# Single attention on one Trainium2 core: the input's statistics one batch further ahead, and its norm moved in front of the residual updates on VectorE

## The reference, cut to what matters

```python
def _layernorm(x, axis=-1, eps=1e-05):
    m = jnp.mean(x, axis=axis, keepdims=True)
    v = jnp.var(x, axis=axis, keepdims=True)
    return (x - m) / jnp.sqrt(v + eps)
...
    q = jnp.einsum('bld,de->ble', query, Wq) + bq
    k = jnp.einsum('bld,de->ble', key, Wk) + bk
    v = jnp.einsum('bld,de->ble', value, Wv) + bv
    scores = jnp.einsum('bqe,bke->bqk', q, k)
    attn = jax.nn.softmax(scores, axis=-1)
    out = jnp.einsum('bqk,bke->bqe', attn, v)
...
    x = _layernorm(x + _L1_attn_ref(x, ...), axis=-1)
    x = _layernorm(x + _L1_xattn_ref(x, ctx_512, ctx_512, ...), axis=-1)
    x = _layernorm(x + _L1_ffn_ref(x, ...), axis=-1)
```

## Time and profile before

| | us |
|---|---|
| median of 3 runs | 2440.24 (2439.1 to 2442.52) |
| the profiled execution, its own time | 2441.61 |
| its span, first to last instruction | 2439.6 |
| PE busy in the span | 2228.2 (91%) |
| VectorE busy | 1570.2 (64%) |
| ScalarE busy | 1121.4 (46%) |
| GpSimd busy | 886.8 (36%) |
| start of the stage's first norm (`E_xn`) and of its last offsets (`E_minus`) | 1935.80 and 2129.07 |
| first instruction of VectorE in the next stage (route) | 2132.88 |

### The profile page before, as it was taken

One profiled execution on the slowest core, in us unless ns is written; L12 is line 12 of the kernel. 1 busy time (PEld: TensorE's weight loads), 2 busy tenths in 40 slices (PEclk: granted clock), 3 DMA queues, 4 the chain that ended last, 5 costly groups with the idle time before them and its releaser, 6 DMA issues. The chain is left out here.

```text
span 2439.6 us, 54300 instructions
## 1 busy us (share of the span) xinstructions
PE 2228.2 (91%) x20297; PEld 1517.8 (62%) x20392; DVE 1570.2 (64%) x3365; ACT 1121.4 (46%) x2397; POOL 886.8 (36%) x1263
## 2 busy tenths in 40 slices
PE   8989999999999997989999999999999699759996
PEld 6656666666666664556666666566666577636664
DVE  2368888788878884746667666666766477652222
ACT  3333333333333331156666666666666277712221
POOL 2111111111111100036666666665665367632442
PEclk9999999999999998989999999999999699959998
DMA  4200000000000001300000000000000022232330
GB/s 147 72 2 2 0 0 0 0 0 0 0 0 0 0 1 50 97 14 0 0 0 0 0 0 0 0 0 0 0 0 1 1 69 89 96 106 91 104 107 24
DMA packets 53289, 65.35 MB, mean 27 GB/s; under 512 B 6257, under 2 KB 46150, under 8 KB 53240
## 3 DMA queue, kind: packets, MB, share of 16 engines
q1 hardware_dynamic: 50168, 56.60, 7.3%
q0 software_dynamic: 3072, 8.07, 1.0%
HBM read 44.01 MB, written 20.97 MB: 27 GB/s over the span
## 5 line engine op out<-in xcount | busy, mean ns | idle before, releaser
L392 PE MATMUL B_ps_s<-B_xk,B_xT 128*32 128x308 f32 x4096 | 278.1, 423 | 9.1 <-DVE B_xk L658 9.1
L1556 DVE TENSOR_TENSOR D_att<-D_ps_s,D_dexp 128x1024 f32<-128x1024 f32 x128 | 154.6, 1208 | 131.2 <-PE D_ps_s L1225 73.3
L413 PE MATMUL B_ps_m<-B_wo,B_oT 128*128 128x256 f32 x1024 | 235.3, 386 | 2.1 <-ACT B_oT L551 2.1
L1126 POOL TENSOR_SCALAR_AFFINE_SELECT D_att<-D_att 128x1024 f32<-128x1024 f32 x128 | 139.9, 1093 | 250.3 <-DVE D_att L1556 250.3
L392 PEld LDWEIGHTS B_ps_s<-B_xk,B_xT 128*32 128x32 f32 x4096 | 129.7, 109 | 142.1 <-issue 13.1
L413 PEld LDWEIGHTS B_ps_m<-B_wo,B_oT 128*128 128x128 f32 x1024 | 192.2, 191 | 39.6 <-issue 12.8
L519 ACT ACTIVATE B_prob<-B_prob 128x616 f32<-128x616 f32 x128 | 92.9, 726 | 241.9 <-DVE B_prob L630 241.9
L308 POOL TENSOR_TENSOR B_veps<-B_mv,eps 128x2 f32<-128x2 f32 x32 | 6.2, 195 | 508.7 <-DVE B_mv L612 508.7
L1134 POOL TENSOR_TENSOR D_orms<-D_oms,D_half 128x32 f32<-128x32 f32 x32 | 174.0, 5436 | 2.7
L1225 PE MATMUL D_ps_s<-D_q2T,D_kT 32*128 32x256 f32 x1024 | 147.7, 404 | 3.7 <-DVE D_att L1556 3.7
L628 DVE TENSOR_REDUCE B_mx<-B_ps_s 128x8 f32<-128x616 f32 x128 | 100.1, 782 | 64.0 <-PE B_ps_s L392 64.0
(11 more groups left out here) (317 smaller groups left out, 4942.8 us busy)
## 6 DMA issues: line engine op xcount, KB each, us to landing
res<-in_x SPq DMA_DIRECT2D x16, 512.0 KB, 3.5
x_d<-res SPq DMA_DIRECT2D x8, 1024.0 KB, 4.5
wi<-in_L_ffn_wi SPq DMA_DIRECT2D x8, 1024.0 KB, 5.0
wo<-in_L_ffn_wo SPq DMA_DIRECT2D x8, 1024.0 KB, 7.5
out<-E_fin SPq DMA_DIRECT2D x7, 1024.0 KB, 7.1
C_wgu<-in_L_ffn_gate_up SPq DMA_DIRECT2D x8, 512.0 KB, 3.6
C_wdn<-in_L_ffn_down_proj SPq DMA_DIRECT2D x8, 256.0 KB, 2.8
B_wqT<-in_L_xattn_WqT SPq DMA_DIRECT2D x1, 1024.0 KB, 11.0
```

The source lines that it names most:

```text
L392: last = nc.tensor.matmul(ps_s[u % 2][q * G:(q + 1) * G, g, 0:HQ * S], xT[:, par, k, (2 * u + g) * G:(2 * u + g + 1) * G], xk[:, par, k].r ...
L413: last = nc.tensor.matmul(ps_m[:, bank, 0:D], oT[:, m, t * P:(t + 1) * P], wo[:, m], start=m == 0, stop=m == MT - 1)
L1126: nc.gpsimd.affine_select(out=att[:, n % 2], in_=att[:, n % 2], compare_op=ALU.is_ge, fill=0.0, base=0, pattern=[[0, HT], [1, P]], channel ...
L1556: nc.vector.tensor_tensor(att[:, n % 2].rearrange("p h i -> p (h i)"), ps_s[:].rearrange("p a n -> p (a n)"), dexp[:, n % 2], ALU.mult).th ...
```

## The change

The statistics of the input are taken at batch b+4, and aggregated and scaled at b+3, where both were at b+2. Input and output statistics get a semaphore each (`stats`, `stats_out`). The first halves of `st` and `mv` are rewritten behind explicit waits: the statistics wait for the last aggregation (`aggr`), the aggregation waits for the norm that still reads `mv` (`xn_ready`). The norm of b+2 moves from the end of VectorE's step to a place in front of the aggregation, ahead of `invert_sums` and `add_out`. GpSimd's order is the same with `norm_scale` numbered one further. Batch 2 gets its aggregation and scales, and batch 3 its statistics, in the prologue. The loop covers steps 3 to 27, and two more steps are written out.

```diff
--- before.py
+++ after.py
@@ -1724,8 +1724,8 @@
         s_out = ps_s[:, 0:NT * (S + E)].rearrange("p (t s) -> p t s", t=NT)
         g_sum, g_v, g_bias, g_bv = (ps_o[:, 1, 64 * n:64 * n + E] for n in range(4))
 
-        set_ready, bias_ready, stats, seen, aggr, var_eps, rstd_ready, xn_ready, resid_ready, ctx_ready = map(
-            sem, "set_ready bias_ready stats seen aggr var_eps rstd_ready xn_ready resid_ready ctx_ready".split())
+        set_ready, bias_ready, stats, stats_out, seen, aggr, var_eps, rstd_ready, xn_ready, resid_ready, ctx_ready = map(
+            sem, "set_ready bias_ready stats stats_out seen aggr var_eps rstd_ready xn_ready resid_ready ctx_ready".split())
         xT_done, k_done, kq_done, v_done, s_done, pT_done, o_done = map(
             sem, "xT_done k_done kq_done v_done s_done pT_done o_done".split())
         gated_ready, g_sum_done, gate_ready, g_v_done, g_v_ready = map(
@@ -1739,12 +1739,12 @@
 
         def steps(engine, body):
             def parts(b):
-                return dict(att=b < B, nxt=b + 1 < B, nxt2=b + 2 < B, sums=1 <= b <= B, x5=2 <= b <= B + 1)
+                return dict(att=b < B, nxt=b + 1 < B, nxt2=b + 2 < B, nxt3=b + 3 < B, nxt4=b + 4 < B, sums=1 <= b <= B, x5=2 <= b <= B + 1)
             for b in range(3):
                 body(b, **parts(b))
-            with engine.Fori(3, B - 2) as b:
-                body(b, att=True, nxt=True, nxt2=True, sums=True, x5=True)
-            for b in range(B - 2, B + 2):
+            with engine.Fori(3, B - 4) as b:
+                body(b, att=True, nxt=True, nxt2=True, nxt3=True, nxt4=True, sums=True, x5=True)
+            for b in range(B - 4, B + 2):
                 body(b, **parts(b))
 
         @block.sync
@@ -1794,13 +1794,13 @@
                 pool.wait_ge(xn_ready, b + 1)
                 nc.gpsimd.tensor_copy(res[:, b], xn[:]).then_inc(resid_ready, 1)
 
-            def body(b, att, nxt, nxt2, sums, x5):
+            def body(b, att, nxt, nxt2, nxt3, nxt4, sums, x5):
                 if nxt2:
                     stage_context(b + 2)
-                if nxt2 or sums:
-                    norm_scale(b + 2, 0 if nxt2 else 1, 2 if sums else 1)
+                if nxt3 or sums:
+                    norm_scale(b + 3, 0 if nxt3 else 1, 2 if sums else 1)
                 if sums:
-                    x5_scales(b - 1, b + 2, first=not x5)
+                    x5_scales(b - 1, b + 3, first=not x5)
                 if nxt2:
                     keep_residual(b + 2)
 
@@ -1814,6 +1814,7 @@
                 norm_scale(b, 0, 1)
                 keep_residual(b)
             stage_context(1)
+            norm_scale(2, 0, 1)
             steps(pool, body)
 
         @block.tensor
...
@@ -1962,16 +1963,23 @@
 
         @block.vector
         def _(dve):
-            def norm_stats(first, last_of):
-                for i, b in enumerate((first, last_of)):
-                    if b is not None:
-                        for t in range(NT):
-                            last = nc.vector.bn_stats(st[:, i, t], res[:, b, t])
-                last.then_inc(stats, 1)
-
-            def norm_aggregate(n, first, last_of):
-                dve.wait_ge(stats, n + 1)
-                dve.sem_inc(seen)
+            def norm_stats(i, b, done):
+                if i == 0 and not (isinstance(b, int) and b == 0):
+                    dve.wait_ge(aggr, b)
+                for t in range(NT):
+                    last = nc.vector.bn_stats(st[:, i, t], res[:, b, t])
+                last.then_inc(done, 1)
+
+            def norm_aggregate(first, last_of):
+                if first is not None:
+                    dve.wait_ge(stats, first + 1)
+                    dve.sem_inc(seen)
+                    if not (isinstance(first, int) and first == 0):
+                        dve.wait_ge(xn_ready, first)
+                        dve.sem_inc(seen)
+                if last_of is not None:
+                    dve.wait_ge(stats_out, last_of + 1)
+                    dve.sem_inc(seen)
                 for i, b in enumerate((first, last_of)):
                     if b is not None:
                         for t in range(NT):
@@ -2018,27 +2026,27 @@
                 nc.vector.scalar_tensor_tensor(minus[:], mv[:, 1, :, 0].unsqueeze(1).to_broadcast([P, 3, NT]), -1.0, scale_n[:],
                                                ALU.mult, ALU.mult).then_inc(minus_ready, 1)
 
-            def body(b, att, nxt, nxt2, sums, x5):
+            def body(b, att, nxt, nxt2, nxt3, nxt4, sums, x5):
                 if att:
                     maxima(b)
-                batches = (b + 2 if nxt2 else None, b - 1 if sums else None)
                 if sums:
                     dve.wait_ge(res_ready, b * NT)
-                if nxt2 or sums:
-                    norm_stats(*batches)
+                    norm_stats(1, b - 1, stats_out)
                 if x5:
                     x5_offsets(b - 2, first=att and b == 2 if isinstance(b, int) else False)
                     dve.wait_ge(minus_ready, b - 1)
-                if nxt2 or sums:
-                    norm_aggregate(b + 2, *batches)
+                if nxt2:
+                    norm_apply(b + 2)
+                if nxt3 or sums:
+                    norm_aggregate(b + 3 if nxt3 else None, b - 1 if sums else None)
                 if att:
                     invert_sums(b)
+                if nxt4:
+                    norm_stats(0, b + 4, stats)
                 if att:
                     add_out(b)
                 if nxt:
                     copy_v(b + 1)
-                if nxt2:
-                    norm_apply(b + 2)
 
             dve.wait_ge(w_loaded, LOADED)
             nc.vector.tensor_tensor(gated[:], gateT[:], gammaT[:].unsqueeze(2).to_broadcast([P, KD, E]), ALU.mult).then_inc(gated_ready, 1)
@@ -2051,9 +2059,12 @@
             dve.wait_ge(gate_ready, 1)
             nc.vector.tensor_copy(kq[:, :, S:S + E], gate[:]).then_inc(bias_ready, 1)
             for b in range(2):
-                norm_stats(b, None)
-                norm_aggregate(b, b, None)
+                norm_stats(0, b, stats)
+                norm_aggregate(b, None)
                 norm_apply(b)
+            norm_stats(0, 2, stats)
+            norm_aggregate(2, None)
+            norm_stats(0, 3, stats)
             dve.wait_ge(g_v_done, 1)
             nc.vector.tensor_copy(wv[:, D:D + E], g_v)
             nc.vector.tensor_copy(bv[:, D:D + E], g_bv[0:S])
```

## The result

The changed kernel takes 2456.34 us (median of 4 runs, 2455.97 to 2457.68), the kernel before 2440.72 us in the same session (4 runs, 2439.1 to 2442.52): a ratio of 1.0064, 95% interval 1.0051 to 1.0077. It is slower, as predicted, but by 15.6 us where 6.8 were forecast, and 2456.3 lies above the range of 2442.0 to 2451.5. The profiled execution took 2457.68 us, span 2455.9 us (before 2439.6).

A forecast was written before the change was run, and what follows sets the result against it. The order of hand-overs, not one engine's work, bounded the 5.61 us step. A new ring of 4.75 + 0.24 + 0.72 + 0.24 = 5.95 us, run 28 times, gave +6.8 us on 2440.24: 2447.0 us, range 2442 to 2451.5.

The forecast's parts named there:

- The bubble: PE's wait of 0.49 us a step for VectorE's normed input, before the input transposes; moving the norm would close it.
- The chain that is left: PE's chain from scores to next scores, 5.42 us a step; if nothing else held, each step would gain 0.19 us.
- a ring through GpSimd: Norm, aggregation, GpSimd's whole step, next norm, in the attention loop: 5.95 us a step, above PE's chain of 5.42.
- the signs named beforehand: Scores every 5.9 us, PE's norm wait gone, its exponential wait larger, GpSimd's aggregation wait 1.3 to 1.5, VectorE newly waiting on GpSimd.
- The tail behind the norm of step 29: After the last ring: norm and hand-over, four chains of aggregation to scales, three hand-overs back; 17.4 us.
- L(1): Start of the norm of step 1, moved from 1951.37 to 1952.33 behind the maxima and two statistics.
- that copy's end to the norm's start: Ring term from the end of GpSimd's residual copy to VectorE's norm: 0.24 us taken, bounds 0.04 and 0.24.
- The second way round: Ring through GpSimd's scales and VectorE's offsets to the norm, 6.09 us or more; rival at +10 to +14 us, 10%.
- Written-out steps: Three ring steps outside the loop, both hand-overs short: 5.75 us each, 17.25 us in the sum.
- The first steps: Attention steps up to about the third would be shorter than 5.6 us.
- The rule on semaphores: If semaphores cost nothing, the non-binding ring would be the forecast; the sum instead followed the trace's 0.15 and 0.24 us gaps.
- The rival on the other side: Hand-overs cost nothing, ring 5.40 us under PE's 5.42, bubble gone: 5.3 us faster, 2435 us; chance 4%.

The follow-up runs named there:

- the kernel with both moves: Changed kernel with GpSimd's residual copy moved in front of the reciprocal root and the norm moved in front of the offsets on VectorE; 2437.88 us, ratio 0.9985.
- the kernel with the copy first: Changed kernel with only GpSimd's residual copy moved from the end of its step to in front of the reciprocal root; 2452.41 us, ratio 1.0051.
- the last kernel: Changed kernel, residual copy first but waiting until the offsets are written, norm ahead of the offsets; 2433.23 us with the loop, 2431.26 us with it written out.
- the kernel with both moves and the copy kept away: Changed kernel, norm ahead of the offsets, residual copy at the head of GpSimd's step but waiting until the offsets are written; 2433.23 us, ratio 0.997.

## Why the prediction was right in direction and wrong in size

**What bounded the kernel before: right.** TensorE's chain, with VectorE's norm in it, set the step there. Writing its loop out gained nothing, and one more power on GpSimd cost 0.11 us a step.

**The bubble: right.** PE's wait for the normed input is gone. The chain that is left was put at 5.42 us; where nothing else binds it is 5.29 us. The term that was off is the copy of K: I took its whole 0.54 us, but its two instructions overlap what follows. In the kernel with both moves the scores start at 1966.06, the copy at 1968.08, the exponential at 1968.51, the transposes of the probabilities at 1969.29 and the next scores at 1971.36: 2.02 + 0.43 + 0.78 + 2.07 = 5.30.

**That a ring through GpSimd binds: right, shown by the runs.** One more power on GpSimd costs 0.53 us a step after the change, 0.11 before it. Its first term, aggregation to the end of the residual copy, was 4.75 us, as predicted. Of the signs named beforehand, VectorE's wait for PE is gone, the new wait stands in front of the offsets, and PE's wait for the exponentials, in no row before, is 8.9 us, as ScalarE's wait for the maxima grew from 5.3 to 20.2 us. The scores come every 6.34 us, not every 5.9; GpSimd's wait for the aggregation, put at 1.3 to 1.5 us a step, is 1.87. The tail behind the norm of step 29 was put at 17.4 us and measured 17.38 (2128.68 to 2146.06); the start, L(1), at 1952.33 and measured 1952.44. All the error lies between: 176.24 us for the 28 rings where the sum has 166.00.

**The step that failed** is "that copy's end to the norm's start ... so I take 0.24". The norm is not the next thing behind the copy. It is the token copy and the offsets, which no semaphore ties to the residual copy, but which end with it. From the copy's end to the norm it is therefore 0.01 + 0.07 + 0.51 = 0.59 us in the loop, 0.35 more than the sum has. With 0.02 on the norm (0.74 for 0.72) and 0.03 on the last hand-over (0.27 for 0.24) that is, but for rounding, the 0.39 us between 6.34 and 5.95. The prediction calls this a ring "with nothing in parallel to it"; scales and offsets lie in parallel to the residual copy, and they bind.

**The second way round** (6.09 us), which I had as the upper bound and as a rival at 10%, was the nearest to the truth: undisturbed it measured 6.19 us, term by term 4.20 + 0.24 + 0.24 + 0.50 + 0.74 + 0.27 (the kernel with the copy first). I compared two branches as if each ran alone and took the shorter, 5.95, for the likelier. Both start from the same aggregation and both must be done before the norm, so the ring is the *longer* of them, and 6.09 was the floor of the forecast, not its ceiling: with 6.09 the sum gives +10.3 us, 2450.5. That is the error of reasoning. The other 0.25 us is the meeting of the two copies (0.15), and 0.10 in four small terms; over 25 loop steps they are 6.3 us, and they, not the choice of the branch, carry the time out of the range. The meeting was in no row of before: there the residual copy and the token copy never met (14.37 to 14.98 and 15.38 after 2000 us).

**Written-out steps.** I put them at 5.75 us; they are 5.88, since there the token copy is held for 0.54 us, which takes back a part of what the shorter hand-over gives.

**The first steps**, from step 1 on, are 5.29 us up to the scores at 1965.64, as predicted ("up to about the third shorter than 5.6"). That VectorE still has lead from the prologue to lose is my reading; no run tests it.

**The rule on semaphores.** The prediction weighed the Trainium skill, page VectorE: DVE Perf Modes, section The DRAIN you can't avoid ("the semaphore costs nothing extra here"), against gaps of 0.15 and 0.24 us. The traces show such gaps from 0.05 to 0.51 us: 0.05 us from the offsets to the norm written out and 0.51 us in the loop, with the same semaphores; 0.26 and 0.27 us from norm to aggregation in either form. Written out is not always short: from the offsets to the aggregation, in the last kernel, it is 0.40 us against 0.48 in the loop. So the rule can hold for the semaphore itself, and the cost lie in the register and semaphore steps between it and the next instruction; which of these steps costs what, no run here separates.

**The rival on the other side** (the ring does not bind, 2435 us) came true in the kernel with both moves and the copy kept away, 2433.2 us, though not by cheaper hand-overs: by an order in which norm and offsets no longer follow one another behind the scales.

## What to carry to other kernels

An operation that is moved in front of a wait inherits that wait, and all that is queued behind it too: before moving, write down for each wait in front of the new place what must have happened since the last step, and take the longest of the branches, not the likeliest. Where GpSimd copies a large tile while VectorE has a short operation on the critical path, look whether they will meet in time after the change; a wait that sends the large copy behind the short operation made the long steps 5.37 us instead of 5.71 here, though GpSimd stands 0.6 us a step for it. And in a loop whose waits are computed in registers, price each hand-over by a row with as many register steps: they counted where the ring bound (9.0 us) and not where it didn't (the kernel before).

## What was unexpected on the hardware

- A copy of 128x2 on VectorE took 0.15 to 0.18 us away from GpSimd's residual copy and 0.33, 0.51 or 0.54 us beside a 128x512 copy on GpSimd that had begun before it, and ended within 0.03 us of it, however early it was issued. The offsets, with two inputs in SBUF, took 0.44 us instead of 0.15 when they came first. VectorE's aggregation was not held beside the same copy (0.38 us from 2012.98, the copy from 2012.88, in the kernel with the copy first), nor was what had begun before it. It goes the other way too: the last of GpSimd's small scales (L1790) took up to 0.43 us instead of 0.20 beside VectorE's norm, in the kernels with both moves. The Trainium skill, page SBUF — State Buffer, section SBUF: two separate sides, says that VectorE and GpSimd share a pair of ports that whichever instruction starts first holds to its end, where the VectorE one runs in a two-port mode or has two inputs in SBUF. The trace agrees for the two copies and for the offsets. It does not bear the rule out for GpSimd's power (next point). The prediction did not use that rule; where copy and copy meet it was worth the remainder of GpSimd's instruction beyond the copy's own time, here 0.15 us a step in the loop.
- In the kernel before, VectorE's norm ran in 0.72 us (2013.12 to 2013.84) inside a power of GpSimd that had begun before it, and the power kept its usual 1.01 us. Yet the added power in the kernel before, which starts 0.03 us ahead of the norm (2013.02 and 2013.05), took 0.80 us instead of 0.55. Either the norm does not take the ports, and then the longer scales and the longer power are unexplained, or a power does not hold them to its end; no run here decides. The row of the first power:

```profile
2012.88 1.01 POOL L1784 TENSOR_TENSOR E_rn<-E_v5eps,E_half 128x4 f32<-128x4 f32 x1
```

- The hand-over from the offsets to the norm, behind the same waits at the same place in the order, measured 0.05 us written out and 0.51 us in the loop. The 0.51 is what two of the loop's gaps of 0.24 had suggested; the 0.05 was not.
- One execution of a stage can have two step lengths in a row (5.29 us seven times, then 5.71 us to the end of the loop), depending on whether two engines' copies meet; the runs of that kernel spread over 12 us, those of the kernel before in the same session over 3.
